# A softmax kernel in which the constant added under the exponential becomes an immediate number

## What is computed

```python
x = x + attn(layernorm(x))
x = x + ffn(layernorm(x))

# attn, for every batch and head
sim  = einsum('bhid,bhjd->bhij', q, k) * 64 ** -0.5
e    = exp(sim - max(sim, -1));  attn = e / (sum(e, -1) + 1e-10)
out  = einsum('bhij,bhjd->bhid', attn, v) ... @ Wo.T + bo

# ffn; fp4(.) rounds to a grid of eight magnitudes, scaled per block of 16
h = silu(fp4(x) @ fp4(w_gate).T) * (fp4(x) @ fp4(w_up).T)
out = fp4(h) @ fp4(w_down).T
```

## Time and profile before

| | |
|---|---|
| median of three timed runs | 1536.53 us (1535.5 to 1538.12) |
| the profiled execution's own time | 1537.8 us |
| its span, first to last instruction | 1535.9 us |
| PE busy | 1465.5 us, 95% |
| POOL busy | 1247.4 us, 81% |
| ACT busy | 1162.8 us, 76% |
| DVE busy | 1090.2 us, 71% |

### The profile page before, as it was taken

One profiled execution on the slowest core, in us unless ns is written; L12 is line 12 of the kernel. 1 busy time (PEld: TensorE's weight loads), 2 busy tenths in 40 slices (PEclk: granted clock), 3 DMA queues, 4 the chain that ended last, 5 costly groups with the idle time before them and its releaser, 6 DMA issues.

```text
span 1535.9 us, 35256 instructions
## 1 busy us (share of the span) xinstructions
PE 1465.5 (95%) x13828; PEld 971.5 (63%) x13828; DVE 1090.2 (71%) x1717; ACT 1162.8 (76%) x2413; POOL 1247.4 (81%) x1391
## 2 busy tenths in 40 slices
PE   4999999999999999999999999999999999999965
PEld 2566666666666666666666666666666666666644
DVE  7666676677667777686776767677676767767567
ACT  3788888877777777777777778777777877777832
POOL 4888989888888888787888878788888888878942
PEclk8999999999999999999999999999999999999987
DMA  6111110101111111111110111111111111111000
GB/s 166 43 42 43 43 42 22 42 23 43 43 42 43 32 35 27 43 43 46 43 26 23 46 43 42 46 28 37 25 46 43 43 43 25 26 42 46 1 4 14
DMA packets 46660, 59.77 MB, mean 39 GB/s; under 512 B 8672, under 2 KB 21920, under 8 KB 46496
## 3 DMA queue, kind: packets, MB, share of 16 engines
q1 hardware_dynamic: 46336, 57.26, 15.9%
q10 hardware_dynamic: 160, 0.26, 0.1%
HBM read 4.80 MB, written 2.10 MB: 4 GB/s over the span
## 4 chain that ended last, share of the span: by engine, by line
PE 81%; DVE 11%; ACT 4%; issue 2%; POOL 1%; DMA 1%; SPq 0%; DVEq 0%
PE ob L633 26%; PE st L605 15%; PE st L607 12%; PE sm L586 10%; PE mb L522 5%; PE mb L538 4%; DVE negm L939 3%; PE mb L527 2%; PE mb L1239 2%; PE mb L533 1%; ACT probs L759 1%; POOL p_low L449 1%; PE mb L1250 1%; PE mb L551 1%; DVE qv L1110 1%
## 5 line engine op out<-in xcount | busy, mean ns | idle before, releaser
L449 POOL TENSOR_TENSOR p_low<-probs 128x512 f16<-128x512 f32 x1024 | 1086.2, 1073 | 226.1 <-ACT probs L759 219.2
L759 ACT ACTIVATE probs<-st,lift,exp_scale 128x512 f32<-128x512 f32 x1024 | 793.4, 775 | 199.9 <-PE st L607 181.1
L939 DVE TENSOR_REDUCE negm<-sm 128x1 f32<-128x1024 f32 x508 | 617.9, 1216 | 162.6 <-PE sm L586 161.2
L605 PE MATMUL st<-q_hl,k_hh 128*128 128x512 f16 x1024 | 393.8, 385 | 2.3 <-DMA q_hm<-m_low 2.3
L607 PE MATMUL st<-q_hm,k_l 128*128 128x512 f16 x1024 | 388.5, 379 | 0.0
L633 PEld LDWEIGHTS ob<-v,p_low 128*128 128x128 f16 x4096 | 275.2, 97 | 123.0 <-POOL p_low L449 3.3
L633 PEld LDWEIGHTS ob<-v,probs 128*128 128x128 bf16 x4096 | 276.1, 98 | 120.7 <-ACT probs L759 0.5
L633 PE MATMUL ob<-v,p_low 128*128 128x129 f16 x4096 | 316.6, 219 | 2.5 <-POOL p_low L449 2.4
L633 PE MATMUL ob<-v,probs 128*128 128x129 f16 x4096 | 317.5, 220 | 0.2
L586 PE MATMUL sm<-k_hh,q_hl 64*128 64x512 f16 x508 | 197.1, 388 | 17.7 <-DVE negm L939 17.7
L586 PE MATMUL sm<-k_hh,q_hm 64*128 64x512 f16 x508 | 197.3, 388 | 0.0
(11 more groups left out here) (175 smaller groups left out, 1539.4 us busy)
## 6 DMA issues: line engine op xcount, KB each, us to landing
k_hh<-k_high SPq DMA_DIRECT2D x128, 128.0 KB, 2.3
k_l<-k_low SPq DMA_DIRECT2D x64, 128.0 KB, 2.3
q_hl<-q_high SPq DMA_DIRECT2D x64, 128.0 KB, 2.3
q_hl<-q_low SPq DMA_DIRECT2D x64, 128.0 KB, 2.4
q_hm<-q_high SPq DMA_DIRECT2D x62, 128.0 KB, 2.3
x<-x SPq DMA_DIRECT2D x4, 512.0 KB, 7.2
q_hm<-m_high SPq DMA_DIRECT2D x128, 1.0 KB
q_hm<-m_low SPq DMA_DIRECT2D x128, 1.0 KB
```

Of the source, the lines that this page charges most:

```text
L449: return pool.tensor_tensor(p_low[b][:, j, :], p, p.bitcast(BF16)[:, 1::2], ALU.subtract)
L605: pe.matmul(st[s % 2][:, :], k_hh[n][:, s * P:(s + 1) * P], q_hl[n][:, half * HALF:(half + 1) * HALF], start=True, stop=False)
L759: nc.scalar.activation(probs[k % 2][:, s, :], st[s % 2][:, :], ACT.Exp, bias=lift[:, 0:1], scale=exp_scale[:, head, pair:pair + 1]).then_i ...
L939: nc.vector.tensor_reduce(negm[k % 2][:, s // 2:s // 2 + 1], banks[:, :, :].rearrange("p a n -> p (a n)"), AX.X, ALU.max, negate=True).the ...
```

## The change

The bias of the Exp is given as the number SCALE * LIFT (8.0) in the instruction. The scale stays a column of `exp_scale`. The number of instructions of every engine, their order and their waits are the same; the tile `lift` is still filled, but nothing reads it.

```diff
-nc.scalar.activation(probs[k % 2][:, s, :], st[s % 2][:, :], ACT.Exp, bias=lift[:, 0:1],
+nc.scalar.activation(probs[k % 2][:, s, :], st[s % 2][:, :], ACT.Exp, bias=SCALE * LIFT,
                      scale=exp_scale[:, head, pair:pair + 1]).then_inc(s_ex, 1)
```

## The result

The changed kernel took 1544.03 us (median of six runs, 1543.09 to 1545.21) against 1537.25 for the kernel before (six runs, 1535.5 to 1538.12). The ratio is 1.0046, with a 95% interval of 1.0033 to 1.0059: slower, by 0.33 to 0.59%. The profiled execution took 1545.21 us with a span of 1543.2.

A forecast was written before the change was run, and what follows sets the result against it. PE was taken as the bound, so only its gaps count. Line 1100 +8.6, kind B -1.4, line 1091 +0.9, other Exps -0.4: +7.7 us, 1545.5 profiled, 1544.2 against the median; own range 1541 to 1547, 8-in-10 range 1535 to 1556.

The forecast's parts named there:

- The price of an operand column: On ACT, one operand column costs an instruction 0.09 us, so the Exp falls from 775 to about 685 ns.
- The order at line 1100: Hidden-layer rounding, 11 places: POOL's p_low starts 0.05 ahead instead of 0.04 behind, so DVE waits; 11 x 0.78 = +8.6 us.
- The other price: If POOL and DVE shared the ports, line 1100 would at most double its 0.52; 0.43 per place, +4.8 us.
- kind B: PE's 0.8 us gap behind layer norm, two Exps and line 1087; shrinks 0.13 each, eleven times, -1.4 us.
- kind A: PE's 0.25 us gap behind hidden-layer rounding (lines 1100, 1125, one Exp, 1110); grows by 0.78, eleven times, +8.6 us.
- the forecast's last paragraph: Signs to look for: PE's gap at the line 1100 places 1.0 us from 0.25, waits for the maximum about 20 from 11.6.
- rival 1: Both orders turn: POOL also overtakes DVE at line 1110, 0.95 later, eleven times 10.5 us; 1554.7 us, chance 0.18.
- Round 5: Line 1091 at 219.87 us falls 0.04 behind POOL and ends at 220.90 instead of 220.05; +0.9 us.
- Rivals 2 and 3: The second: no order turns, 1533.6 us, chance 0.20. The third: the number saves nothing, 1536.5 us, chance 0.12.
- rival 2: No order turns between POOL and DVE; only chains shrink, -2.9 us, 1533.6 us, chance 0.20.

The follow-up runs named there:

- one_exp_of_round: Against the kernel before, bias a number in only 11 of the 1024 Exps, slot (0, 4) of rounds that round a hidden layer; 1546.37 us, ratio 1.0061.
- operand_at_weights_too: Against the kernel after, the bias operand kept in those 11 Exps of hidden-layer rounding and all Exps of rounds 5, 7 and 8; 1533.69 us, ratio 0.9978.

## Why the prediction was right, point by point

The forecast was 1544.2 us and slower; 1544.03 was measured. The mechanism, POOL overtaking DVE at line 1100, is what happened. That the two times agree to 0.2 us is in part luck. The forecast was 7.7 us above a median of 1536.53, and the result is 6.8 above one of 1537.25; and a term that was missing nearly cancels one that was too small.

- **The price of an operand column.** Taken as 0.09 us, an Exp of about 685 ns; the Exp takes 686, 0.089 less.
- **The order at line 1100.** Forecast: POOL 0.05 ahead, line 1100 at about 1.4 us, p_low at 1.04. All eleven are so, at 1.38 us. The other price, +4.8 by sharing (11 x 0.43 is 4.7), is ruled out by the same 1.38.
- **Its price.** The delay of line 1100 was put at 0.87 and one_exp_of_round measures 0.86 us of PE for it. In the kernel after, the odd rounds grew by 0.62; with kind B's 0.15 taken out of that, kind A costs 0.77, where the sum had 0.78. How it reaches PE was told only in part. The wait at the sm matmul before (0.25 at 760.17) was named, the one of line 533 for q_low was not. PE works in order, so both are parts of the same delay and the last wait takes what is left: it is 0.39 and not the 1.0 of the forecast's last paragraph. For the same reason PE's waits for the maximum came to 14.6 us and not to 20.
- **The order at line 1110** (rival 1). A lead of 0.02 was forecast, and 0.02 it is; DVE kept it in all eleven repeats, so the rival fell.
- **Kind B.** Forecast 0.13 and no more; PE's gap there shrank by 0.12, and the round in which it stands by 0.15. The round behind it gained 0.07, which the sum lacked: it looked at no place where DVE was held and might come free, and line 1110 of the 256-column rounding is one. Over twelve rounds of each sort that is -2.6 instead of -1.4 us.
- **Round 5.** Line 1091 at 220 us was forecast to come 0.04 behind POOL and to end 0.85 later. It takes 1.04 us instead of 0.18, and the round is 0.99 longer. From the timeline of all engines after:

```profile
220.59 1.04 POOL L449 TENSOR_TENSOR p_low<-probs 128x512 f16<-128x512 f32 x1 [0.18 <-ACT probs L759]
220.62 1.04 DVE L1091 TENSOR_SCALAR q_small<-q_small 128x24 f32<-128x24 f32 x1
```

- **What was missed: round 8.** Line 1087 at 355 us is held too, and the round is 1.08 us longer. The sum looked for places where POOL was to come in front by the recorded starts, and here it doesn't, as the last section shows. This term and kind B's shortfall (-1.2) nearly cancel.
- **Sum from the rounds.** 11 x 0.62 + 0.99 + 1.08 - 0.8 - 0.2 = 7.9 us, against a forecast of 7.7 and a difference of medians of 6.8. The rest is no more than what the traces differ by ahead of the first Exp and behind the last.
- **Rivals 2 and 3** fell with the profile: the order turned, and the Exp is shorter. The gain that rival 2 saw is real, though, and somewhat larger than its 2.9 us: operand_at_weights_too, in which POOL doesn't overtake DVE at line 1100 or in rounds 5 and 8, is 4.0 us below the kernel before beside it (3.6 by its rounds). Part of that is the 0.07 of each even round, which rival 2 didn't have.

## What to carry to other kernels

A faster instruction off the critical path can cost more than it saves when it sets the start of work on an engine that shares something with a third one. Before shortening it, list the places where its follower starts just behind an instruction that it excludes: a margin smaller than the time saved is a turn of the order, and its price is nearly the follower's whole duration (0.86 us here, for a p_low of 1.04), not the margin of 0.05. If the order turns, look for an idle gap of the held engine ahead of that place, and move the step there: this took the loss away here and brought a gain of its own. List the places where the second engine is held already, too: the same shortening can free it there, as it did at line 1110 of the 256-column rounding.

## What the runs showed of the hardware

With POOL idle beforehand, the recorded starts decided in the cases read here: POOL ahead by 0.03 (220.59 against 220.62), 0.05 and 0.14 us held DVE, DVE ahead by 0.02 or 0.04 held POOL. The Trainium skill, "SBUF — State Buffer", section "Who interferes with whom", gives the rule of the first to issue, and these rows agree with it. Where POOL's instruction follows another of its own without a break, who is held doesn't follow from the recorded starts. Two cases of the kernel after; the first from the timelines of POOL alone and of all engines, the second from that of all engines:

```profile
354.61 0.47 POOL L456 TENSOR_TENSOR o_n<-oscl 128x128 f32<-128x128 f32 x1
355.02 3.22 POOL L449 TENSOR_TENSOR p_low<-probs 128x512 f16<-128x512 f32 x3
```
```profile
354.95 1.15 DVE L1087 TENSOR_SCALAR q_small<-q_small 128x22 f32<-128x22 f32 x1
```
```profile
700.92 0.45 POOL L456 TENSOR_TENSOR o_n<-oscl 128x128 f32<-128x128 f32 x1
701.33 2.41 POOL L449 TENSOR_TENSOR p_low<-probs 128x512 f16<-128x512 f32 x2
701.44 0.40 DVE L1110 SCALAR_TENSOR_TENSOR qv<-qw,qv 128x256 f32<-128x256 f32 x1
```

In the first, line 1087 starts 0.07 before p_low, during POOL's instruction before, and still stands until p_low is done: 1.15 us for 22 columns. In the kernel before it started 0.15 before its p_low (353.43), also during POOL's instruction before, and took 0.25 (timeline of DVE alone):

```profile
353.28 0.25 DVE L1087 TENSOR_SCALAR q_small<-q_small 128x22 f32<-128x22 f32 x1
```

In the second, line 1110 starts 0.11 after p_low and is not held (0.40; in the kernel before it started 0.25 after p_low and took 1.06), while p_low and the next one take 2.41 us together, where two undisturbed ones take 2 x 1.04 less their overlap of 0.04. In both p_low's recorded start lies some 0.04 before the end of the instruction ahead of it. So behind a running instruction of the same engine the recorded start isn't the moment that decides; what is, these runs leave open. It was not tried apart.
